# Third layer's attention on the tokens: each head's scores from its own 32 rows, without the masked copies of the keys

## The reference, cut to what matters

```
def _mha(x, y, wq, wk, wv, li1_w, li1_b, ..., causal):      # H, D = 16, 32; here x = y = _ln(xx, ln1_g, ln1_b)
    xn = _ln(x, lnx_g, lnx_b);  yn = _ln(y, lny_g, lny_b)
    q = jnp.einsum('bsc,hcd->bhsd', xn, wq)
    k = jnp.einsum('btc,hcd->bhtd', yn, wk)
    v = jnp.einsum('btc,hcd->bhtd', yn, wv)
    a = jax.nn.softmax(jnp.einsum('bhsd,bhtd->bhst', q, k) * D ** (-0.5), axis=-1)
    if causal:
        a = a * (t > s)                       # after the softmax: weights of earlier tokens are dropped
    o = jnp.einsum('bhst,bhtd->bhsd', a, v)
    o = o.transpose(0, 2, 1, 3).reshape(x.shape[0], x.shape[1], H * D)
    x_out = x + o @ li1_w + li1_b
```

## Time and profile before

| | |
|---|---|
| time of the runs, median of 3 | 5869.38 us (5861.38 to 5875.85) |
| time of the profiled execution | 5845.47 us |
| its span, first to last instruction | 5843.6 us |
| stage l3a in it | about 3506 to 4457 us |
| busy share of the span: PE, DVE, ACT, POOL | 84%, 72%, 47%, 36% |
| one round of l3a in its steady stretch | 14.58 us |

### The profile page before, as it was taken

One profiled execution on the slowest core, in us unless ns is written; L12 is line 12 of the kernel. 1 busy time (PEld: TensorE's weight loads), 2 busy tenths in 40 slices (PEclk: granted clock), 3 DMA queues, 4 the chain that ended last, 5 costly groups with the idle time before them and its releaser, 6 DMA issues. The chain is left out here.

```text
span 5843.6 us, 134152 instructions
## 1 busy us (share of the span) xinstructions
PE 4882.0 (84%) x40251; PEld 3691.1 (63%) x40251; DVE 4188.7 (72%) x10467; ACT 2757.5 (47%) x5756; POOL 2105.6 (36%) x2536
## 2 busy tenths in 40 slices
PE   7888998999942996088879998888888799998898
PEld 5666567888842564066657665777776577776544
DVE  7887775777765332288876767888887699997544
ACT  4554674555520332055555544555554355554344
POOL 3332000011037001643333336777776633333300
PEclk9998998999975998599989998999999899998988
DMA  0000500000011343100000000000000000000000
GB/s 33 2 2 21 230 0 16 5 5 5 5 59 43 131 139 102 48 3 2 2 13 1 0 0 9 0 0 0 0 0 6 7 2 2 2 2 6 1 13 16
DMA packets 113844, 136.89 MB, mean 23 GB/s; under 512 B 45016, under 2 KB 88216, under 8 KB 108956
## 3 DMA queue, kind: packets, MB, share of 16 engines
q1 hardware_dynamic: 105504, 118.30, 6.1%
q0 software_dynamic: 8192, 16.79, 1.0%
HBM read 44.85 MB, written 58.72 MB: 18 GB/s over the span
## 5 line engine op out<-in xcount | busy, mean ns | idle before, releaser
L1881 POOL TENSOR_TENSOR l3a_probs<-l3a_probs,l3a_later 128x512 f32<-128x512 f32 x256 | 320.7, 1283 | 4.9 <-DVE l3a_total L2069 4.9
L1867 POOL TENSOR_TENSOR l3a_keys<-l3a_kT,head 128x2048 f32<-128x2048 f32 x64 | 230.5, 3601 | 232.5 <-ACT l3a_kT L1994 232.5
L1296 POOL DMA_INDIRECT l1c_rows<-l_rows,l1f_slots x128 | 122.2, 955 | 443.8 <-PEq L1288 403.3
L359 POOL TENSOR_TENSOR l0x_keys<-l0x_kT,head 128x1232 f32<-128x1232 f32 x64 | 145.1, 2268 | 354.7 <-ACT l0x_kT L446 354.7
L359 POOL TENSOR_TENSOR l2x_keys<-l2x_kT,head 128x1232 f32<-128x1232 f32 x64 | 145.1, 2267 | 321.1 <-ACT l2x_kT L444 321.1
L1929 PE MATMUL l3a_scores<-l3a_keys,l3a_qT 128*128 128x512 f32 x512 | 256.5, 604 | 4.2 <-POOL l3a_keys L1867 4.2
L166 POOL TENSOR_TENSOR l1x_ve<-l1x_mv,eps 128x1 f32<-128x1 f32 x64 | 12.3, 191 | 656.1 <-DVE l1x_mv L158 656.1
L294 PE MATMUL l3a_po<-l3a_vals,l3a_probsT 128*128 128x32 f32 x2048 | 248.1, 269 | 0.1
L294 PEld LDWEIGHTS l3a_po<-l3a_vals,l3a_probsT 128*128 128x128 f32 x2048 | 247.1, 192 | 0.4 <-ACT l3a_probsT L275 0.4
L250 ACT ACTIVATE l3a_probs<-l3a_probs 128x512 f32<-128x512 f32 x256 | 161.7, 632 | 180.5 <-DVE l3a_probs L241 175.5
L1367 POOL TENSOR_TENSOR l2f_hid<-l2f_prod,l2f_route 128x512 f32<-128x512 f32 x128 | 152.2, 1194 | 255.3 <-DVE l2f_prod L1514 242.2
(11 more groups left out here) (520 smaller groups left out, 17315.5 us busy)
## 6 DMA issues: line engine op xcount, KB each, us to landing
l_rows<-l0f_zeros SPq DMA_DIRECT2D x34, 1024.0 KB, 25.9
l1f_parts<-l1f_split SPq DMA_DIRECT2D x40, 512.0 KB, 3.6
l1e_x_in<-l_rows SPq DMA_DIRECT2D x40, 256.0 KB, 2.8
l1f_down<-l1f_w SPq DMA_DIRECT2D x40, 256.0 KB, 2.4
l_rows<-l1e_y_out SPq DMA_DIRECT2D x40, 256.0 KB, 2.7
l1f_w<-in_L_W SPq DMA_DIRECT2D x16, 256.0 KB, 3.2
out_x<-x_res SPq DMA_DIRECT2D x16, 256.0 KB, 2.0
x_res<-in_x SPq DMA_DIRECT2D x1, 3840.0 KB, 12.6
```

The costliest lines, as they stand in the source:

```text
L359: pool.tensor_tensor(keys[it.par][:, :, :], kT[it.par][:, :].unsqueeze(1).to_broadcast([P, HEADS, KEYS]), g.head8[:, :].unsqueeze(2).to_br ...
L1296: pool.indirect_dma_start(rows[p][:, k * P:(k + 1) * P], None, g.xs[:, :], bass.IndirectOffsetOnAxis(ap=slots[:, it.b * CHOICES + k:it.b * ...
L1867: pool.tensor_tensor(keys[it.par][:, :, :, :], kT[it.par][:, :, :].unsqueeze(2).to_broadcast([P, J, G4, T]), g.head32[:, :].unsqueeze(1).u ...
L1881: pool.tensor_tensor(v, v, later[:, :].unsqueeze(1).to_broadcast([P, 4, T]), ALU.mult).then_inc(s_masked, 1)
```

## The change

In `l3a` alone the masked copies go. `spread` and the buffer `keys` are not made, and POOL's list of steps begins with deviation3. The scores of a head are now a product over its own 32 rows of qT and kT, 128 columns wide, so 16 products of a batch stand where 4 stood. A bank now holds the four heads with the same 32 rows (h mod 4 = r) instead of the four of a column group, and two banks are written in turn: `score01` writes banks 0 and 1 by turns, `score23` banks 2 and 3. The heads' new places are followed up in the values (`natural`) and in the division, which stays one instruction. `fetch_k` waits for the scores of two batches ago instead of for `keys`. Stage `l3c` is as before.

```diff
+        def natural(h):
+            return G4 * (h % J) + h // J if first else h
...
-                steps = {"spread": (spread, 3), "deviation3": (lambda it: n3.inverse_deviation(pool, it), 2 if first else 1)}
+                steps = {"deviation3": (lambda it: n3.inverse_deviation(pool, it), 2 if first else 1)}
                 if first:
...
-                    names = "spread deviation3 deviation2 deviation1 drop0 drop1 drop2 drop3"
+                    names = "deviation3 deviation2 deviation1 drop0 drop1 drop2 drop3"
...
+                def score_rows(it, c):
+                    pe.wait_ge(s_kT, nth(it))
+                    pe.wait_ge(s_qT, nth(it))
+                    if (due := nth(it, 4, c + 1, back=4)) is not None:
+                        pe.wait_ge(sm.s_shift, due)
+                    for j in range(J):
+                        for r in (c, c + 1):
+                            rows = slice(D * r, D * r + D)
+                            last = pe.matmul(scores[r][:, j * T:(j + 1) * T], qT[it.par][rows, j, :], kT[it.par][rows, j, :],
+                                             start=True, stop=True)
+                            if j == J - 1:
+                                last.then_inc(sm.s_scores, 1)
...
-                        cols = slice(h * D, (h + 1) * D)
+                        cols = slice(natural(h) * D, (natural(h) + 1) * D)
...
-                    sm.times_values(pe, it, c, lambda h: po[:, h * D:(h + 1) * D], values_of)
+                    sm.times_values(pe, it, c, lambda h: po[:, natural(h) * D:(natural(h) + 1) * D], values_of)
...
                 if first:
-                    names = ("score0 turn_o turn score1 score2 turn_p0 output queries score3 keys turn_p1 weigh0 turn_p2 weigh1 "
+                    steps.update(score01=(lambda it: score_rows(it, 0), 4), score23=(lambda it: score_rows(it, 2), 4))
+                    names = ("score01 turn_o turn turn_p0 output queries score23 keys turn_p1 weigh0 turn_p2 weigh1 "
                              "turn_p3 weigh2 weigh3 values")
...
-                    if (due := nth(it, ago=2)) is not None:
+                    if first:
+                        if (due := nth(it, 4, ago=2)) is not None:
+                            act.wait_ge(sm.s_scores, due)
+                    elif (due := nth(it, ago=2)) is not None:
                         act.wait_ge(s_keys, due)
...
+                    if first:
+                        dve.tensor_tensor(o_s[p][:, :].rearrange("p (j r d) -> p j r d", r=G4, d=D),
+                                          po[:, :].rearrange("p (j r d) -> p j r d", r=G4, d=D),
+                                          recip[p][:, :].rearrange("p (r j) -> p j r", j=J).unsqueeze(3).to_broadcast([P, J, G4, D]),
+                                          ALU.mult).then_inc(s_o, 1)
+                        return
```

More of the change, by code:

```diff
@@ L1807, in l3_attention @@
         qT, kT, vals = st.sb2("qT", [P, J, P]), st.sb2("kT", [P, J, T]), st.sb2("vals", [T, HEADS * D])
-        keys = st.sb2("keys", [P, J, G4, T])
         if not first:
+            keys = st.sb2("keys", [P, J, G4, T])
             vhi, vlo = st.sb2("vhi", [T, HEADS * D], F16), st.sb2("vlo", [T, HEADS * D], F16)
@@ L1886, in _ @@
                                  deviation2=(lambda it: n2.inverse_deviation(pool, it), 1), **numbered("drop", drop_earlier, 4, 4))
-                    names = "spread deviation3 deviation2 deviation1 drop0 drop1 drop2 drop3"
+                    names = "deviation3 deviation2 deviation1 drop0 drop1 drop2 drop3"
                 else:
-                    steps.update(deviation_y=(lambda it: ny.inverse_deviation(pool, it), 2), begin_y=(begin_y, 4))
+                    steps.update(spread=(spread, 3), deviation_y=(lambda it: ny.inverse_deviation(pool, it), 2), begin_y=(begin_y, 4))
                     names = "deviation_y spread deviation3 begin_y"
@@ L1956, in output @@
                     last.then_inc(s_y, 1)
-                steps = {**numbered("turn_p", turn_p, 4, 5), **numbered("score", score, 4, 4), **numbered("weigh", weigh, 4, 5),
+                steps = {**numbered("turn_p", turn_p, 4, 5), **numbered("weigh", weigh, 4, 5),
                          "turn": (turn, 3), "queries": (queries, 3), "keys": (keys_of, 3), "values": (values, 3),
@@ L1961, in _ @@
                 if first:
-                    names = ("score0 turn_o turn score1 score2 turn_p0 output queries score3 keys turn_p1 weigh0 turn_p2 weigh1 "
+                    steps.update(score01=(lambda it: score_rows(it, 0), 4), score23=(lambda it: score_rows(it, 2), 4))
+                    names = ("score01 turn_o turn turn_p0 output queries score23 keys turn_p1 weigh0 turn_p2 weigh1 "
                              "turn_p3 weigh2 weigh3 values")
                 else:
+                    steps.update(numbered("score", score, 4, 4))
                     names = ("turn_p0 score0 turn_p1 turn score1 turn_o queries output turn_p2 score2 weigh0 turn_p3 keys "
```

## The result

The kernel after takes 6034.9 us (median of 4 runs, 6023.4 to 6036.4), the kernel before, on the same chip, 5868.9 (5861.4 to 5875.9). The ratio is 1.028 [1.0267, 1.0293]: 166 us slower, where I had forecast 64.

A forecast was written before the change was run, and what follows sets the result against it. DVE was taken to set the 14.58 us round. Early drops, +69 us, less 5 for the filling, gave +64: 5869.4 + 64 = 5933 us for the median, range of 8 in 10 5862 to 5968.

The forecast's parts named there:

- DVE sets the round, PE stands still 1.5 us before the keys: Stage l3a before the change: DVE sets the 14.58 us round; PE waits 1.5 us for ACT's copy of the queries.
- The early drops: POOL's drops start before DVE's hat and hold DVE's instructions: net +1.14 us per round, +69 us over 61 rounds.
- The alternation: After each held DVE instruction POOL gets its turn, so DVE's next one waits for a whole POOL instruction.
- The first normalization gets back 0.44: DVE's first normalization of stats2 comes after the drops are over and saves 0.44 us per round.
- Filling, -5 us: Without POOL's copy, PE no longer waits for it twice while the stage fills: gain 4 to 7 us, taken as 5.
- PE's products, 3.6 us a batch: PE's 16 small score products take 3.6 us per batch instead of 3.4, bounds 1.8 to 8.7, hidden in its spare time.
- Rival 4: PE's pause grows to about 2.4 us, or 4, and its clock falls: +0.3 us per round, 18 us, 5951 us; chance 12%.

The follow-up runs named there:

- e5: Kernel after with three full products (128 rows, 512 columns) that nobody reads put into PE's pause before the keys; 5932.7 us, ratio 1.0138.
- g9: Kernel after, but POOL still makes the masked copies, unread, and two full products that nobody reads fill PE's pause before the keys; 5861.0 us, ratio 1.0013.
- g10: e4 with one full product that nobody reads put before the keys on PE; 5869.8 us, ratio 1.0033.
- h16: e8 with ACT's copy of the queries moved ahead of its first fetch and first exponential; 5826.5 us, ratio 0.9937.
- e4: Kernel after with POOL's drops one round later, between DVE's held instructions, and PE's turn of group 0 behind score23; 6315.8 us, ratio 1.0756.
- e8: Kernel before, copies and products kept, with only POOL's list changed so the drops come first, behind the division's addition; 5878.8 us, ratio 1.0043.
- e3: Kernel after with each small product of the scores made twice into the same place; 6068.4 us, ratio 1.0321.
- h14: e4 with ACT's copy of the queries moved ahead of its first fetch and first exponential, without a filling product; 5927.0 us, ratio 1.0097.

## Why the prediction was wrong in size

- *DVE sets the round, PE stands still 1.5 us before the keys.* Right.
- *The early drops: +1.14 us a round, 15.7.* Right: 15.72 - 14.55 = 1.17 in e5, and +79 us against before, where 69 was the term without the filling; over g9, whose drops are late, e5 loses 69. The alternation read in the earlier trace rows carried over to the hat, the renormalization and the multiplication.
- *The first normalization gets back 0.44.* Right: 337 ns (L1785 from x).
- *Filling, -5 us.* Not seen: the stage starts at the low clock, and 3530 to 3640 us ran at 0.65 (0.95 before).
- *PE's products, 3.6 us a batch.* Too high. Half a batch took 1.16 us with its overhang of 0.16, so 2.0 a batch, near the lower bound of 1.8. As time off the path that cost nothing; but the pause it left was 3.0 us, not 2.4 (4 was the figure for row groups that overlap).
- *Rival 4, slower by the clock, +0.3 us a round.* This step failed. The sum had no term for the clock; the rival named the fall and its pause, but gave it 12% and a price from the short stretch of another stage. Falls of that length, 3.4 us, do occur, but more than half of the falls last 17 to 20.5 us, a whole round. Why they last so long is open: PE was busy for 19.67 of the 19.70 us in the row above. I also let the delay hide behind the held hat; instead the hat wasn't held, and DVE waited 3.77 us before its division. Measured: 166 - 79 = 87 us on top of the held instructions, or 160 by itself, for 18 forecast.
- *What I had no term for:* the new products count far less than full ones for the clock. Before, 3.4 us of full products stood where 2.0 us over 32 rows stand now, so the pause is longer and what is left of the scores holds the clock less.

What stays open: which mixture of pauses and light work the clock bears. One filler didn't hold it in the kernel after, one did in g10. h16 shows that falls come without a pause and without narrow rows too. Products over 64 rows were not tried.

## What to carry to other kernels

Before making PE's work smaller or narrower, look at its pause and at the rows of its products: what a stall behind another engine hides as time may not be hidden as clock, and a fall costs whole rounds. Price a clock's fall from the round it slows, not from the length of a stretch elsewhere. When POOL's load goes, see where its remaining work lands beside DVE's two-input and normalizing instructions, and move it by its waits; here the order gave 0.6%, and the new products with a filler at most 0.2 to 0.4 beside it.

## What the runs showed of the hardware

- One full product more in each round took 432 us off (e4 to g10, 451 and 19 us over the kernel before), and the clock went from 0.64 to 1.00. In e4 PE was 89% busy; the clock came back again and again and fell each time.
- Of 26 falls in the kernel after twelve lasted 3.4 us and fourteen 17 to 20.5, with PE busy all through the one that was looked at (19.67 of 19.70 us).
- Three products of 512 columns a round hold the clock over 128 rows and not over 32 (1.00 and 0.85, 5932.7 and 6039.2 us). A pause of 1.8 us a round left it at 1.00 with full products (e8); with narrow ones it fell at pauses of at most 1.6 (e3) and 0.7 us (h14).
- The clock can fall with PE never idle for long and all products over 128 rows (h16, 0.96, PE busy 99%).
- Eight products of 32 rows by 128 columns on alternating rows take 1.16 us, 1.71 with four in a row on the same rows: that is 0.0625 us a record instead of the 0.1125 of full products. The kernel alternates two groups of rows, and two banks with them, so what four at once would take wasn't seen.
